# First stage of a decoder layer: squared norms taken in pairs on two column strips, the last chunk reordered, and the loads of the second heads moved to the sync queue

## The chip, the cores and the metric

The kernel runs on one core of a Trainium2 chip. The metric is the device time of one launch in microseconds (us), lower is better. The core has TensorE (matmul, PE), VectorE (DVE), ScalarE (ACT), GpSimd (POOL) and SyncE (SP). They run side by side and meet at semaphores. SP and ACT also issue DMAs here, each on a queue of its own; the data is moved by 16 DMA engines.

## What is computed

One post-norm decoder layer on x of shape (4, 1024, 256): self-attention with a positional bias, cross-attention to 77 context rows, and a top-2 of 8 experts block, each followed by a residual and a layer norm. What matters here is the first stage, the projections of the self-attention:

```python
qkv = jnp.einsum('bsd,ed->bse', x, Wqkv)
q, k, v = jnp.split(qkv, 3, axis=-1)          # 16 heads of 16
logits = jnp.einsum('bihd,bjhd->bhij', q, k) * scale + pos_bias[None]
attn = jax.nn.softmax(logits, axis=-1)
```

The softmax needs an upper bound of each logit in place of its true maximum. The kernel uses |q|·max|k|: for every query row the norm of q (the "norm row" that is stored beside q), and one maximum of |k| over all keys, turned into a shift row of the keys.

## The kernel before

The first stage (`front`) goes over 4096 tokens in eight chunks of 512 (`CH`, c = 0 to 7). In each chunk TensorE computes four units (`unit(c, u)`, line 312): u = 0, 1 are the two halves of K, u = 2, 3 the two halves of Q, each 128 rows by 512 tokens with two accumulation steps, in float32. Each unit has a PSUM bank of its own (`ps_u[u]`). It is drained like this:

- ScalarE copies it to bfloat16 (`parts[u][:, 0]`, "hi", line 434), squares it (`squares[u]`, line 435), and VectorE subtracts hi from it (`rest[u]`, line 502). ScalarE turns the rest to bfloat16 ("mid", line 385), GpSimd takes what is left ("lo", line 585). The mid of a unit comes after the hi and the square of the next one (`finish`).
- SyncE stores hi, mid and lo of each unit to `kstack` or `qstack` (line 229). The hi copy of the same unit of the next chunk waits until all these stores have landed (`unit_stored[u]`).
- TensorE sums the squares by head with a small bfloat16 matmul, `norm(c, u)` (line 322): `members` (128 x 8) are its weights, the squares its 512 moving columns, 8 partitions of PSUM its output. For K, VectorE takes the maximum over the 512 tokens (`key_peak`, line 507); for Q, ScalarE takes the root (line 388) and SyncE stores it as the norm row of 8 partitions (line 233). There are two PSUM banks for norms, `ps_n[u % 2]`, so K and Q take turns in each.

TensorE's order in a chunk is: unit 0, extra work (`fills(c, 0)`, small matmuls of the positional table and of the cross-attention), unit 1, norm 0, unit 2, `fills(c, 1)`, norm 1, unit 3, norm 2, V of the first 256 tokens (`values(c, 0)`, line 339), norm 3, V of the others (`values(c, 1)`). VectorE copies the V results out (`copy_values`, line 513), and SyncE stores them (line 238).

The last chunk also closes the bound on the keys. VectorE writes an early shift row into both key buffers (`early_rows`, line 542, two instructions on one partition with 4096 elements each), then takes the last maxima, the maximum of all (line 560); TensorE turns it over (`key_bound`, line 347), VectorE reduces it (line 571), TensorE spreads it (`spread_bound`, line 352), ScalarE takes the root (line 444), VectorE makes the shift row (lines 575, 577). `key_bound` stands ahead of `values(7, 0)` and `spread_bound` ahead of `values(7, 1)` in TensorE's order.

Self-attention follows without a barrier, head group by head group, 8 steps of 128 keys for each 512 queries. Its first step needs the queries, keys and values of the first heads, the root of the key bound, and free PSUM; the second step on VectorE, ScalarE and GpSimd after that (s = 2) waits for `front_stored`, that is, until all of the first stage's stores have landed. Its output banks `ps_o` are zeroed by VectorE at its start (line 738); they lie where the banks of the norms were.

ScalarE's queue also issues the loads that prefetch the attention (`prefetch(c, u)`): the bias strips and factors in chunks 2 to 5, the seven query loads of the first heads (lines 66 and 84) in (5, 3), their six key loads in (6, 1), their values in (6, 3); and of the second heads the queries in (7, 1), the keys and the values in (7, 3).

## Time and profile before

| | us |
|---|---|
| median of 3 runs | 1292.52 (1290.61 to 1292.66) |
| the profiled execution, its own time | 1292.1 |
| its span in the trace | 1289.9 |
| first stage: TensorE's first matmul to the end of its last `values` | 7.44 to 131.35 |
| TensorE busy over the whole span | 1180.4 (92%) |
| VectorE, ScalarE, GpSimd busy | 860.3, 794.2, 775.4 |

The first stage is a tenth of the span. The engine shares over the whole span are an average over self-attention, cross-attention, routing and experts, so the first stage is read by itself: in stretches of one chunk, each from TensorE's first matmul of the chunk to that of the next.

### The profile page before, as it was taken

How to read it: one execution, taken by the hardware profiler on the slowest of the kernel's cores; microseconds unless marked ns; L12 is line 12 of the kernel's file. 1: busy time of each engine (PE TensorE's matmuls, PEld its weight loads, DVE VectorE, ACT ScalarE, POOL GpSimd, SP SyncE). 2: the span in 40 equal slices, each digit the busy share in tenths (PEclk: the TensorE clock that was granted, in tenths of full speed). 3: DMA queues.
4: the chain of work that ended last, by engine and by line, in shares of the span. 5: the costliest groups of instructions: out<-in, count | busy, mean ns of one | idle time of the engine just before them, and what ended most of it. 6: DMA issues, size and time to landing. Idle time of an engine off the chain costs nothing.

```text
span 1289.9 us, 28208 instructions
## 1 busy us (share of the span) xinstructions
PE 1180.4 (92%) x10751; PEld 682.3 (53%) x10751; DVE 860.3 (67%) x1473; ACT 794.2 (62%) x948; POOL 775.4 (60%) x516
## 2 busy tenths in 40 slices
PE   7999999999999999999899999439999999999980
PEld 3444233333333333332345453339999999999980
DVE  3454789999989999998557886724444444444445
ACT  4555799999999999999376657302222222222224
POOL 1233688878888788888246887734445444444433
PEclk9999899999999999999899999669999999999995
DMA  7699645485559553462277862977777777777748
GB/s 223 201 318 287 235 76 76 76 259 85 90 88 270 83 88 84 71 136 73 84 181 195 216 182 99 188 237 237 243 240 244 235 235 236 245 239 244 237 111 264
DMA packets 134222, 232.51 MB, mean 180 GB/s; under 512 B 31609, under 2 KB 80542, under 8 KB 133766
## 3 DMA queue, kind: packets, MB, share of 16 engines
q1 hardware_dynamic: 102432, 178.10, 46.9%
q0 software_dynamic: 25024, 39.74, 16.4%
q10 hardware_dynamic: 6630, 12.82, 3.4%
q8 instruction: 90, 1.47, 0.5%
q14 instruction: 46, 0.38, 0.1%
HBM read 103.91 MB, written 52.76 MB: 121 GB/s over the span
## 4 chain that ended last, share of the span: by engine, by line
PE 68%; DVE 13%; POOL 5%; issue 5%; ACT 4%; DMA 2%; SPq 0%; ACTq 0%; DVEq 0%; POOLq 0%
PE xp_ps_h L2421 20%; PE xp_ps_y L2433 9%; PE sa_sum L711 9%; PE sa_o L725 9%; DVE sa_probs L759 8%; PE sa_factor L711 4%; PE qp_ps L312 4%; POOL sorted L1136 2%; PE qp_ps L339 2%; ACT sa_probs L783 1%; PE cb_misc L1290 1%; PE cb_l L1305 1%; DVE sa_o_out L745 1%; PE xp_ps_x L2410 1%; ACT fi_rows L2547 1%
## 5 line engine op out<-in xcount | busy, mean ns | idle before, releaser
L807 POOL TENSOR_TENSOR sa_probs<-sa_probs,sa_factors 128x1024 f32<-128x1024 f32 x160 | 383.8, 2399 | 98.0 <-ACT sa_probs L777 98.0
L759 DVE TENSOR_TENSOR sa_probs<-sa_sum,sa_strips 128x1024 f32<-128x1024 f32 x352 | 413.0, 1217 | 44.0 <-PE sa_sum L711 43.7
L783 ACT ACTIVATE sa_probs<-sa_probs 128x1024 f32<-128x1024 f32 (+1 forms) x256 | 342.9, 1384 | 1.2 <-DVE sa_probs L759 1.2
L2421 PEld LDWEIGHTS xp_ps_h<-arena,big 128*128 128x128 f32 x2272 | 266.2, 193 | 5.1 <-ACT arena L2451 1.6
L2421 PE MATMUL xp_ps_h<-arena,big 128*128 128x128 f32 x2272 | 266.8, 276 | 0.9 <-ACT arena L2451 0.9
L725 PE MATMUL sa_o<-sa_probs,sa_v 128*17 128x512 f32 x2048 | 265.7, 594 | 0.8 <-POOL sa_probs L807 0.6
L2389 POOL DMA_INDIRECT y_sum<-stage,xp_place_of x71 | 114.4, 1612 | 190.7 <-DVE xp_weight_of L2480 89.2
L711 PE MATMUL sa_sum<-sa_qk 97*32 97x512 bf16 x2816 | 201.7, 383 | 12.0 <-DVE sa_probs L759 5.2
L711 PEld LDWEIGHTS sa_sum<-sa_qk 97*32 97x32 bf16 x2816 | 63.4, 95 | 230.2 <-DVE sa_probs L759 129.9
L777 ACT ACTIVATE sa_probs<-sa_factor 128x1024 f32<-128x1024 f32 x160 | 164.1, 1026 | 7.0 <-PE sa_factor L711 7.0
L2433 PE MATMUL xp_ps_y<-big,arena 128*128 x568 | 134.5, 380 | 1.3 <-DVE arena L2488 1.3
L2461 ACT ACTIVATE stage<-arena,xp_weight_of 128x256 f32<-128x256 f32 x71 | 36.1, 508 | 129.1 <-DVE arena L2497 129.1
L2433 PEld LDWEIGHTS xp_ps_y<-big,arena 128*128 128x128 f32 x568 | 102.4, 190 | 12.7 <-issue 1.7
L2451 ACT ACTIVATE arena<-xp_ps_x 128x256 f32<-128x256 f32 x71 | 27.2, 383 | 123.7 <-PE xp_ps_x L2410 123.7
L711 PE MATMUL sa_factor<-sa_qk 97*32 97x512 bf16 x1280 | 98.5, 384 | 0.3 <-ACT sa_probs L777 0.3
L2479 DVE CAST xp_place_of<-arena 128x1 uint32<-128x1 f32 x71 | 10.9, 154 | 131.5 <-PE xp_ps_h L2421 131.5
L2378 POOL DMA_INDIRECT arena<-sorted,ro_row_of x71 | 70.2, 989 | 40.3 <-issue 27.5
L585 POOL TENSOR_TENSOR qp_parts<-qp_rest,qp_parts 128x512 bf16<-128x512 f32 x32 | 36.9, 1157 | 89.9 <-ACT qp_parts L385 89.9
L725 PEld LDWEIGHTS sa_o<-sa_probs,sa_v 128*17 128x17 f32 x2048 | 55.8, 99 | 58.4 <-ACT sa_probs L783 3.6
L2482 DVE TENSOR_TENSOR arena<-xp_ps_h,arena 128x1024 f32<-128x1024 f32 x71 | 86.2, 1214 | 0.0
L2455 ACT ACTIVATE arena<-arena 128x512 f32<-128x512 f32 x71 | 44.8, 631 | 65.1 <-DVE arena L2482 65.1
L1470 ACT ACTIVATE big<-cb_l,arena 77x1024 f32<-77x1024 f32 x64 | 68.4, 1106 | 25.4 <-PE cb_l L1305 21.6
(249 smaller groups left out, 1284.9 us busy)
## 6 DMA issues: line engine op xcount, KB each, us to landing
big<-big SPq DMA_DIRECT2D x142, 512.0 KB
sa_strips<-line SPq DMA_DIRECT2D x3, 3840.0 KB, 16.5
sa_qk<-qstack SPq DMA_DIRECT2D x84, 128.0 KB
sa_qk<-kstack SPq DMA_DIRECT2D x84, 128.0 KB
oT<-sa_o_out SPq DMA_DIRECT2D x32, 256.0 KB, 2.4
kstack<-qp_parts SPq DMA_DIRECT2D x48, 128.0 KB, 3.8
qstack<-qp_parts SPq DMA_DIRECT2D x48, 128.0 KB
sa_factors<-factor_line SPq DMA_DIRECT2D x3, 1920.0 KB, 20.5
```

The costliest lines, as they stand in the source:

```text
L711: last = nc.tensor.matmul(into[c * KEYS:(c + 1) * KEYS, a, :], k[m % 2][:, h, at:at + KEYS], q[m % 2][:, h, ih * CH:(ih + 1) * CH], start= ...
L725: last = nc.tensor.matmul(ps_o[n % 2][32 * h:32 * h + VW, :], v[m % 2][:, jt, VW * h:VW * (h + 1)], probs[s % RING][:, h, :], start=(jt == ...
L759: nc.vector.tensor_tensor(probs[s % RING][:, 2 * half:2 * half + 2, :], ps_sum[sums_before(s, half) % 2][:, :, :], strips[hg % 2][:, 2 * h ...
L777: nc.scalar.activation(probs[s % RING][:, 2:4, :], ps_factor[:, :, :], ACT.Exp, scale=0.25).then_inc(factor_exp, 1)
L783: nc.scalar.activation(probs[s % RING][:, 0:heads, :], probs[s % RING][:, 0:heads, :], ACT.Exp, scale=0.25).then_inc(exp_done, 1)
L807: nc.gpsimd.tensor_tensor(probs[s % RING][:, 2:4, :], probs[s % RING][:, 2:4, :], factors[hg % 2][:, :, c1 - CH:c1][:, :, ::-1], ALU.mult) ...
L1470: nc.scalar.activation(pT[:, first:first + 3:2, :], ps_l[use % 2][:NK, :, :], ACT.Exp, bias=neg_shift[:NK, 0:1], scale=HD ** -0.5).then_in ...
L2378: pool.indirect_dma_start(out=x[s % XRING][:, 0:ROW].bitcast(I32), out_offset=None, in_=io["sorted"], in_offset=bass.IndirectOffsetOnAxis( ...
L2389: pool.indirect_dma_start(out=io["y_sum"], out_offset=bass.IndirectOffsetOnAxis(place_of[:, s:s + 1], 0), in_=y[s % 2][:, :], in_offset=No ...
L2421: last = nc.tensor.matmul(ps_h[parity % 2][:, n, m * P:(m + 1) * P], w_now[s % WRING][:, n, k, m * P:(m + 1) * P], xT[parity % 2][:, k, :] ...
L2433: last = nc.tensor.matmul(ps_y[parity % 2][:, 0:D], g[parity % 2][:, k, :], w2[:, e, k, :], start=(k == 0), stop=(k == KH - 1))
L2482: nc.vector.tensor_tensor(h[i][:, :, :].rearrange("p n (m c) -> p (n m) c", c=P), ps_h[i][:, :, :].rearrange("p n (m c) -> p (n m) c", c=P ...
```

## The change

Four things are altered together, all in the first stage and at its seam with the attention.

1. Norms by pairs. `members` becomes 128 x 32 (its pattern repeated), and `norm(c, j)` does the two units 2j and 2j+1 in two matmuls to partitions 0 to 31 and 32 to 63 of one bank `ps_n[j]`, K in bank 0 and Q in bank 1. One `reduce_max` and one root, each over 64 partitions, take the place of two. TensorE's order becomes unit 0, fills, unit 1, unit 2, norm 0, fills, unit 3, V first part, norm 1, V second part. The norm rows of both Q halves are stored after all parts of unit 3.
2. In the last chunk VectorE takes the maximum of all right after its one key maximum, writes one early row before and one after `subtract(7, 2)`, and reduces the turned maximum before `subtract(7, 3)`.
3. The attention's output banks are allocated outside both stages and shared with the norms. They are zeroed by VectorE in the last chunk, after the last root; the shift row follows, and then `copy_values(7, 1)`, which before stood ahead of both.
4. The loads of the second heads (queries, keys, values: 14 DMAs) are issued by SyncE after `front_stored` and ahead of the wait for the shift row, and no longer by ScalarE in chunk 7.

```diff
-        members = sb("members", [P, 8], BF16)
+        members = sb("members", [P, 32], BF16)
-        norms = [sb(f"norms{u}", [8, CH], BF16) for u in range(2)]
+        norms = sb("norms", [64, CH], BF16)
-        ps_n = [ctx.enter_context(nc.psum_tensor(f"qp_norm{u}", [P, CH], F32)) for u in range(2)]
+        ps_n = sa["ps_o"]
@@ SyncE, store(c)
-                    if u >= 2:
-                        sp.wait_ge(root_done, 2 * c + u - 1)
-                        sp.dma_start(dst[NORM_ROW * 8:NORM_ROW * 8 + 8, bass.ts(c, CH)],
-                                     norms[u - 2][:, :]).then_inc(unit_stored[u], 16)
+                sp.wait_ge(root_done, c + 1)
+                for i in range(2):
+                    sp.dma_start(io["qstack"][i][NORM_ROW * 8:NORM_ROW * 8 + 8, bass.ts(c, CH)],
+                                 norms[32 * i:32 * i + 8, :]).then_inc(unit_stored[2 + i], 16)
@@ TensorE
-            def norm(c, u):
-                pe.wait_ge(sq_done, 4 * c + u + 1)
-                if u >= 2:
-                    pe.wait_ge(peak_done, 2 * c + u - 1)
-                elif c >= 1:
-                    pe.wait_ge(root_done, 2 * (c - 1) + u + 1)
-                nc.tensor.matmul(ps_n[u % 2][0:8, :], members[:, :], squares[u][:, :],
-                                 start=True, stop=True).then_inc(norm_ready, 1)
+            def norm(c, j):
+                pe.wait_ge(sq_done, 4 * c + 2 * j + 2)
+                if c >= 1:
+                    pe.wait_ge((peak_done, root_done)[j], c)
+                for i in range(2):
+                    last = nc.tensor.matmul(ps_n[j][32 * i:32 * i + 32, :], members[:, :], squares[2 * j + i][:, :],
+                                            start=True, stop=True)
+                last.then_inc(norm_ready, 1)
                 unit(c, 1)
-                norm(c, 0)
                 unit(c, 2)
+                norm(c, 0)
                 fills(c, 1)
-                norm(c, 1)
                 unit(c, 3)
-                norm(c, 2)
                 if c == NCH - 1:
                     key_bound()
                 values(c, 0)
-                norm(c, 3)
+                norm(c, 1)
@@ ScalarE
-                if u >= 2:
-                    act.wait_ge(norm_ready, 4 * c + u + 1)
-                    nc.scalar.activation(norms[u - 2][:, :], ps_n[u % 2][0:8, :], ACT.Sqrt).then_inc(root_done, 1)
+                if u == 3:
+                    act.wait_ge(norm_ready, 2 * c + 2)
+                    nc.scalar.activation(norms[:, :], ps_n[1][0:64, :], ACT.Sqrt).then_inc(root_done, 1)
-                elif (c, u) == (7, 1):
-                    rows_stored(1)
-                    load_queries(act, io, sa, 1)
-                elif (c, u) == (7, 3):
-                    load_keys(act, io, sa, 1)
-                    load_values(act, io, sa, 1)
@@ VectorE, in the loop over c
                 subtract(c, 1)
                 if c == NCH - 1:
-                    early_rows()
-                key_peak(c, 0)
+                    early_shift()
+                    early_row(0)
+                key_peak(c)
+                if c == NCH - 1:
+                    dve.wait_ge(peak_done, NCH)
+                    nc.vector.reduce_max(k_top[0:64, 0:1], k_peak[:, :], AXX).then_inc(bound_done, 1)
                 subtract(c, 2)
                 drains(c, 1)
-                key_peak(c, 1)
                 if c == NCH - 1:
-                    dve.wait_ge(peak_done, 2 * NCH)
-                    nc.vector.reduce_max(k_top[0:8, 0:1], k_peak[:, :], AXX).then_inc(bound_done, 1)
+                    early_row(1)
+                    dve.wait_ge(kmax_mm, 1)
+                    nc.vector.reduce_max(k_top[0:1, 1:2], ps_u[0][0:1, 0:64], AXX).then_inc(bound_done, 1)
                 subtract(c, 3)
+                copy_values(c, 0)
                 if c == NCH - 1:
                     cross_shift()
-                    dve.wait_ge(kmax_mm, 1)
-                    nc.vector.reduce_max(k_top[0:1, 1:2], ps_u[0][0:1, 0:8], AXX).then_inc(bound_done, 1)
-                for n in range(2):
-                    copy_values(c, n)
...
+                    dve.wait_ge(root_done, NCH)
+                    for bank in ps_n:
+                        nc.vector.memset(bank[:, :], 0.0).then_inc(sa["emptied"], 1)
+                    dve.wait_ge(bound_done, 5)
+                    nc.vector.tensor_scalar(k_top[:, 3:4], k_top[:, 2:3], -1.05, None, ALU.mult).then_inc(bound_done, 1)
+                    dve.wait_ge(bound_done, 6)
+                    nc.vector.tensor_scalar(sa["shift_row"][ROWS:ROWS + 1, :], ones_row[ROWS:ROWS + 1, 0:S],
+                                            k_top[ROWS:ROWS + 1, 3:4], None, ALU.mult).then_inc(bound_done, 1)
+                copy_values(c, 1)
@@ self_attention, SyncE
+            load_queries(sp, io, sa, 1)
+            load_keys(sp, io, sa, 1)
+            load_values(sp, io, sa, 1)
             sp.wait_ge(sa["bound_done"], 7)
             load_bias(1)
@@ self_attention, VectorE
-            for n in range(2):
-                nc.vector.memset(ps_o[n][:, :], 0.0).then_inc(emptied, 1)
```

The waits of `key_bound` and of the first attention steps are as before; the turned maximum is 64 wide instead of 8.

## Rows read from the trace of the kernel before

**Rows 1.** Windows, chunks 5 and 7: length, busy by engine, PEclk, DMA share, GB/s

```profile
86.75:99.74 12.99, 12.99 (x42) 6.16 (x41) 5.58 (x10) 6.46 (x13) 3.47 (x3) 1.00 1.01 347
112.81:131.35 18.54, 15.94 (x41) 7.85 (x39) 8.88 (x14) 9.17 (x17) 5.56 (x6) 0.83 1.04 260
```

**Rows 2.** Waits of TensorE, 0 to 135 us: total, times, longest

```profile
PE qp_norm L322 <- DVE qp_k_peak L507: 1.6, 1, 1.6
PE qp_ps L347 <- DVE qp_k_top L560: 1.0, 1, 1.0
```

**Rows 3.** Timeline of TensorE, chunk 7: start, length, instructions, idle before

```profile
112.81 3.60 PE L312 MATMUL qp_ps<-qp_x,qp_w 128*128 128x512 f32 x8
116.34 0.38 PE L322 MATMUL qp_norm<-qp_squares,qp_members 128*8 128x512 bf16 x1
116.65 1.98 PE L312 MATMUL qp_ps<-qp_x,qp_w 128*128 128x512 f32 x4
118.56 0.38 PE L322 MATMUL qp_norm<-qp_squares,qp_members 128*8 128x512 bf16 x1
```

**Rows 4.** Timeline, TensorE in the attention, eight matmuls on four column strips

```profile
168.54 0.60 PE L711 MATMUL sa_factor<-sa_qk 97*32 97x512 bf16 x8
168.97 1.03 PE L725 MATMUL sa_o<-sa_probs,sa_v 128*17 128x512 f32 x8
```

**Rows 5.** Timeline of TensorE, end of chunk 7

```profile
122.42 0.38 PE L322 MATMUL qp_norm<-qp_squares,qp_members 128*8 128x512 bf16 x1 [1.57 <-DVE qp_k_peak L507]
123.95 2.73 PE L339 MATMUL qp_ps<-qp_w,qp_x 128*128 128x256 f32 x8
127.64 3.78 PE L339 MATMUL qp_ps<-qp_w,qp_x 128*128 128x256 f32 x8
```

**Rows 6.** Windows of 1 us around both falls of the clock, columns as in Rows 1

```profile
126.00:127.00 1.00, 1.00 (x3) 0.08 (x1) 0.28 (x1) 0.60 (x1) 0.00 (x0) 0.50 1.08 277
134.00:135.00 1.00, 0.00 (x0) 0.00 (x0) 1.00 (x1) 0.00 (x0) 0.89 (x1) 1.00 0.05 17
136.00:137.00 1.00, 0.83 (x12) 0.30 (x12) 1.00 (x2) 0.21 (x1) 0.47 (x1) 0.50 0.73 123
```

**Rows 7.** Timeline of VectorE, chunk 7 and the seam

```profile
118.35 3.21 DVE L542 TENSOR_SCALAR sa_qk<-qp_ones_row,qp_k_early 1x4096 bf16<-1x4096 bf16 x2
121.60 0.68 DVE L507 TENSOR_REDUCE qp_k_peak<-qp_norm 8x1 f32<-8x512 f32 x1
131.46 0.69 DVE L513 COPY qp_v_out<-qp_ps 128x512 f32<-128x512 f32 x1 [4.06 <-PE qp_ps L339]
132.84 1.02 DVE L738 MEMSET sa_o<- 128x512 f32 x2
133.90 4.80 DVE L759 TENSOR_TENSOR sa_probs<-sa_sum,sa_strips 128x1024 f32<-128x1024 f32 x4
```

**Rows 8.** Timeline of ScalarE: chunk 5, a wait and its followers; chunk 7

```profile
91.59 0.60 ACT L434 ACTIVATE qp_parts<-qp_ps 128x512 bf16<-128x512 f32 x1 [1.38 <-DMA kstack<-qp_parts]
92.09 0.59 ACT L435 ACTIVATE qp_squares<-qp_ps 128x512 bf16<-128x512 f32 x1
120.14 0.60 ACT L434 ACTIVATE qp_parts<-qp_ps 128x512 bf16<-128x512 f32 x1 [2.09 <-issue]
```

**Rows 9.** Timeline of SyncE's queue, stores of the norm rows of chunk 4

```profile
85.73 0.41 SPq L233 DMA_DIRECT2D qstack<-qp_norms  x1
88.18 0.34 SPq L233 DMA_DIRECT2D qstack<-qp_norms  x1
```

**Rows 10.** Landing of line 229's K stores; DMA issues at 87 to 90, 128 to 133

```profile
DMA to landing us min/median/max: 1.9/3.8/8.4
...
kstack<-qp_parts SPq DMA_DIRECT2D x1, 128.0 KB, 7.0
...
vpad<-qp_v_out SPq DMA_DIRECT2D x2, 272.0 KB, 4.2
```

**Rows 11.** Timeline of GpSimd, the first product of the attention

```profile
134.11 2.36 POOL L807 TENSOR_TENSOR sa_probs<-sa_probs,sa_factors 128x1024 f32<-128x1024 f32 x1 [5.85 <-ACT sa_probs L777]
```

49 lines of the change are left out of this document (23 added, 26 removed).

## Prediction

> **What bounds the kernel now.** I read the change first, to know which stretch it can touch (the first stage and its seam with the attention), and then the windows by chunk [rows 1]. The reader is to see that in chunk 5 TensorE's busy time is the whole length of the stretch (12.99 of 12.99), while VectorE, ScalarE and GpSimd are at half of it or less. Chunks 0 to 4 and 6 look the same; only chunk 7 has idle TensorE time (15.94 of 18.54) and a mean granted clock of 0.83. Next the waits of TensorE [rows 2]: over the whole first stage it waits for an engine only twice, 1.6 and 1.0 us, both in chunk 7. So in chunks 0 to 6 a microsecond that TensorE doesn't spend is a microsecond of the end time, as long as nothing else becomes late; in chunk 7 the chain through VectorE counts too. The other number to watch is the DMA share, 1.01 in chunk 5 and 1.04 in chunk 7: the 16 engines have no room there, and this is where the cover may fail. Later stages start from semaphores and not from a date, so I carry a gain of the first stage to the end unchanged.
>
> **What one norm costs.** Two units back to back and the step to the norm take 116.34 - 112.81 = 3.53 us [rows 3]. Eight matmuls of 0.43 us make 3.44, so 0.09 is the step into the narrow matmul. The norm takes 116.65 - 116.34 = 0.31. The unit behind it takes 118.56 - 116.65 = 1.91, and of that 0.09 is again the step into the next norm, so 0.10 beyond 1.72 is the step out. One norm costs 0.09 + 0.31 + 0.10 = 0.50 us of TensorE. Four a chunk: 2.0.
>
> **What a pair costs.** It has one step in, one step out, and two streams of 512 columns. Bounds: if the two strips run together it costs what one does, 0.50; if one after the other, the second adds a stream of 0.21 (half of a float32 matmul's 0.43). The nearest row has bfloat16 matmuls of 512 columns on four column strips: eight start at 168.54 and the next line's at 168.97, 0.43 for two rounds of four [rows 4]. Strips run together there, at 0.21 a round, and I take 0.02 for the second strip: 0.52. A pair of norms saves 2 x 0.50 - 0.52 = 0.48, two pairs a chunk 0.96, and chunks 0 to 6 give 7 x 0.96 = 6.7 us (serial strips: 4.0).
>
> The Trainium skill ("TensorE: Matmul & The Clock Gate", the table of measured speedups in the part on packing small matmuls) has a less perfect figure for column strips: three strips of 512 columns ran 2.38 times as fast as one by one, 1.26 of a single one's time. By that a pair would cost some 0.05 us more than I take, an estimate from that page, and the sum would lose under 1 us. The rows of this kernel show no such loss, and the sum keeps to them.
>
> **What else of the pairs is free, and its cover.** The pair needs the second unit's squares. They end about 1.1 us after the unit (hi at 91.59, square 92.09 to 92.68 [rows 8]), and a unit of 1.72 lies between: covered, by 0.5. The pair for Q has `values(c, 0)` as the same cover. Eight roots and eight key maxima (0.68 us each [rows 7]) go away, on engines that are not the bound: nothing. Their replacements run over 64 partitions instead of 8 with the same 512 elements each, so I give them the same length.
>
> **The stores of the norm rows, where I see a loss.** Before, the row of unit 2 is issued ahead of unit 3's parts (85.73) and that of unit 3 behind them (88.18) [rows 9], 1.0 before and 1.4 us after chunk 5 begins at 86.75. Now both go last, that of unit 2 at about +1.4. The hi copy of unit 2 in the next chunk waits for this row, and it is due earlier than before: three units (5.2) and the fill of chunk 5 (0.6, what 12.99 leaves beside six times 1.72 and four norms [rows 1]), about +5.8. That leaves 4.4 us to land. A store of a K part lands in 3.8 us in the median, which fits; one issued at 87 to 90 took 7.0, and the longest 8.4 [rows 10]. So in chunk 5 I expect the hi copy at about +8.3, 2.5 us late. Queued behind it on ScalarE are square 2, mid 1, hi 3 and square 3, half a microsecond apart: square 3 ends at 8.3 + 0.5 x 4 + 0.6 = 10.9. TensorE comes to the Q pair at about +9.8 (four units 6.9, fill 0.6, pair 0.5, V 1.8). It stalls 1.1 us. A wait for a landing of this kind is already there once, 1.38 us on ScalarE [rows 8]. In chunk 6 the first heads' key loads keep ScalarE to about +7.3 anyway and the landing is near it; I take 0.4 more for chunks 4 and 6 together. Range of this term: 0 to 5 us. I take 1.5.
>
> **Chunk 7, counted from its first matmul (112.81).** Before, two things make VectorE late: ScalarE's six query loads and one row load hold back hi 2 to 120.14 [rows 8], and the two early rows take 3.21 us ahead of the key maximum (121.60 [rows 7]). TensorE waits twice for this [rows 2], and then its clock is 0.50 instead of 1.00 [rows 6]: `values` take 2.73 and 3.78 where 1.99 is usual [rows 5]. It ends at 131.35, +18.5, and the attention's first add starts at 133.90, +21.1.
> After: TensorE does units 0 to 2 (5.2), the pair (to 5.6), unit 3 (to 7.5). VectorE has subtract 1 until 5.4, the early shift 0.15, one early row 1.6 (to 7.15), the key maximum to 7.85, the maximum of all to 8.05. `key_bound` starts there: TensorE waits 0.6. Then V first part to 10.0, the Q pair to 10.5. VectorE has meanwhile subtract 2 (8.7), the other early row (10.35), the turned maximum (10.5), and `spread_bound` waits 0.1 at most. V second part: 10.8 to 12.7. So TensorE saves 18.5 - 12.7 = 5.8: 2.6 - 0.7 of idle time, 2.9 of low clock (0.8 + 1.9 in `values`, the rest in the small ones), and 1.0 of norms.
> VectorE goes on with subtract 3 (11.3), V copy (11.9), then waits for the last root. ScalarE has mid 3 at 11.4 to 12.0 and the root to 12.5. Zeroing takes 1.02 [rows 7], to 13.5; the key root is ready at 12.7; the shift row 0.6, to 14.2; the second V copy 0.7, to 14.9. The first add starts at about +14.95. The seam is 2.2 us after TensorE's end where it was 2.5. The gain to the first add is 21.1 - 14.95 = 6.1 us.
>
> **Who waits for the V copy.** It was the first of this row of steps and is now the last. The first factor scores of TensorE and the last V store wait for it. The scores come at +15.0, about when the first add starts; before, they came ahead of it. Their exponential (1.0) and GpSimd's product (2.36 [rows 11]) end near +19, and TensorE wants them with the values of step 0 at about +20: covered by 1 us. The store takes about 4.2 to land [rows 10], so `front_stored` comes at about +19; three adds of 1.2 end at +18.6. A new wait of 0.4 (0 to 1.5) on VectorE.
>
> **The second heads' loads.** What they cost ScalarE in chunk 7 is counted above. On SyncE they stand behind `front_stored` and ahead of the shift row's wait and of the bias of head group 1. 14 issues of some 0.5 are 7 us, so they are out at about +26, and step 16 wants them 30 us after the first add, +45. The bias is wanted at step 64. SyncE's first output store is due at about +38. Nothing: covered by over 10 us each. The DMA engines do the same work, only later.
>
> **Start of the attention.** Before, TensorE idles at 133 to 135 us and the clock falls again [rows 6]. It still has about 1.5 to 2 us idle between +13.3 and +15. I expect one fall there as before: no difference; 2 us less if it doesn't come.
>
> **Sum.** -6.7 (pairs) + 1.5 (rows that land late) - 6.1 (chunk 7 and seam) + 0.4 (`front_stored`) = -10.9 us. The profiled execution's own time is 1292.1 (span 1289.9 and 2.2 around it), 0.4 below the median of the runs, so 1292.1 - 10.9 = 1281.2, and 1281.6 against the median. I give 1281.5.
>
> **The rivals.**
> - A: the DMA engines take more of it back. For it: the share over 1.0 [rows 1] and 7.0 us to landing, while every chunk is now 1 us shorter. If chunks 4 to 7 stall 1 to 1.5 us each, the term is 5: 1285. Against: ScalarE has about 1.5 us of slack before TensorE feels it. Chance 0.18.
> - B: strips one after another, or dearer steps in and out because of the 32-column weights. 2.7 us less, 1 more in chunk 7: 1284.5 to 1285. Against: [rows 4]. Chance 0.07.
> - C: chunk 7 still trips the clock. TensorE's idle 0.7 there is small beside the 2.6 that stood before the fall, but if ScalarE or a landing makes it 2, the 2.9 us stay and 1 or 2 of idle time with them: 1285 to 1286. Chance 0.12.
> - D: better than the sum. No late rows (1.5) and no fall at the start of the attention (2): 1278. Chance 0.15.
> - E, slower than before: the late rows drag the clock down. Place: hi of unit 2 in chunks 4 to 7. If every norm row took 8.4 us (the longest landing [rows 10]), the hi copy would be 4 us late, TensorE would stall 2.4, as long as the 2.6 before the fall in chunk 7, and the stretch behind it would run at half clock, which cost 2.9 there. Four times 5.3 is 21, less 12.8: +8, 1300. It decides from a stall of about 2 us in three chunks on. Against: the median of 3.8. Chance 0.04.
> - F: it does its part but the end doesn't move, since a later stage waits for something with a date of its own. I see none. Chance 0.03.
>
> **How the numbers follow.** The forecast has 0.41. The range reaches from D without its last half microsecond to A, B and most of C: 1277.5 to 1286, and leaves out E, F and the tails. A difference of 0.2% (2.6 us) is about what a measurement of this kernel can tell. Faster by over 0.2%: all but E, F and a worse form of A or C, 0.91. Within: 0.05. Slower: 0.04.
>
> **What would show it.** The windows by chunk should be near 12.0 us for chunks 5 and 6, with TensorE's norm rows as two matmuls 128*32 starting within 0.05 us of each other. Chunk 7 should take 12.7 with a clock of 1.00. A wait of ScalarE's line 434 for `qstack` stores, or of TensorE's norm for ScalarE's square, in chunk 5 or 6, shows the late rows. On VectorE the order is zeroing, shift row, V copy, first add without gaps. I am wrong if the chunks keep 13 us without TensorE idle (B), if TensorE idles over 1 us in several chunks (A, E), or if the clock row shows 0.50 before +12 of chunk 7 (C).

## The result and the profile after

The changed kernel takes 1280.32 us, median of 7 runs (1278.53 to 1286.26), beside 1292.52 (1290.61 to 1297.39) before: a ratio of 0.991, 95% interval 0.9887 to 0.9932. The forecast was 1281.5 with a range of 1277.5 to 1286.0. The profiled execution took 1281.3 us (span 1279.5), 10.8 less than that of before (1292.1, span 1289.9).

Windows of the changed kernel, chunks 5, 6 and 7, columns as in [rows 1]:

```profile
82.06:94.28 12.22, 12.19 (x41) 6.19 (x40) 4.96 (x9) 5.78 (x11) 3.65 (x4) 1.00 1.03 349
94.28:107.70 13.42, 12.23 (x42) 6.54 (x41) 4.77 (x9) 8.00 (x15) 5.08 (x5) 1.00 1.08 322
107.70:120.95 13.25, 12.29 (x45) 6.28 (x47) 8.97 (x15) 7.87 (x15) 7.13 (x7) 1.00 0.68 226
```

Chunk 5 went from 12.99 to 12.22 with TensorE still busy throughout (12.19). Chunk 6 has 1.2 us without TensorE. Chunk 7 went from 18.54 to 13.25, and its clock is 1.00 where it was 0.83. Its DMA share is 0.68 where it was 1.04.

Timeline of TensorE, chunks 6 and 7 and the seam, beside [rows 3] and [rows 5]:

```profile
100.60 0.39 PE L323 MATMUL sa_o<-qp_squares,qp_members 128*32 128x512 bf16 x2 [0.28 <-ACT qp_squares L429]
105.54 0.39 PE L323 MATMUL sa_o<-qp_squares,qp_members 128*32 128x512 bf16 x2 [0.91 <-ACT qp_squares L429]
...
107.70 5.31 PE L314 MATMUL qp_ps<-qp_x,qp_w 128*128 128x512 f32 x12
112.94 0.39 PE L323 MATMUL sa_o<-qp_squares,qp_members 128*32 128x512 bf16 x2
113.26 1.98 PE L314 MATMUL qp_ps<-qp_x,qp_w 128*128 128x512 f32 x4
116.21 0.27 PE L349 MATMUL qp_ps<-arena,qp_k_top 64*1 64x64 f32 x2 [0.96 <-DVE qp_k_top L553]
116.41 1.99 PE L341 MATMUL qp_ps<-qp_w,qp_x 128*128 128x256 f32 x8
...
118.96 1.99 PE L341 MATMUL qp_ps<-qp_w,qp_x 128*128 128x256 f32 x8
...
122.74 0.61 PE L714 MATMUL sa_factor<-sa_qk 97*32 97x512 bf16 x8 [1.24 <-DVE qp_v_out L507]
```

A pair is one line with x2, and what follows starts 0.32 us later (112.94 to 113.26) where one norm took 0.31. Both `values` of chunk 7 take 1.99 instead of 2.73 and 3.78. The last line is new: the first factor scores wait for the V copy, which now comes last on VectorE.

Timeline of VectorE, chunk 7 and the seam, beside [rows 7]:

```profile
113.23 2.01 DVE L537 TENSOR_SCALAR sa_qk<-qp_ones_row,qp_k_early 1x4096 bf16<-1x4096 bf16 x1
115.28 0.68 DVE L501 TENSOR_REDUCE qp_k_peak<-sa_o 64x1 f32<-64x512 f32 x1
116.00 0.15 DVE L553 TENSOR_REDUCE qp_k_top<-qp_k_peak 64x1 f32<-64x8 f32 x1
...
116.78 1.28 DVE L537 TENSOR_SCALAR sa_qk<-qp_ones_row,qp_k_early 1x4096 bf16<-1x4096 bf16 x1
...
120.36 1.02 DVE L572 MEMSET sa_o<- 128x512 f32 x2 [0.67 <-ACT qp_norms L388]
...
122.71 4.80 DVE L760 TENSOR_TENSOR sa_probs<-sa_sum,sa_strips 128x1024 f32<-128x1024 f32 x4
```

The first add starts 11.19 us earlier than before (133.90 to 122.71). Four adds run without a gap, so VectorE doesn't wait for `front_stored`.

Where the gain arises and where it stays:

| change, us | forecast | measured |
|---|---|---|
| chunks 0 to 6, TensorE's work | -6.7 | -6.3 |
| TensorE's waits in them | +1.5 | +1.2 |
| chunk 7 and the seam, to the first add | -6.1 | -6.1 |
| from the first add to the attention's last output copy | +0.4 | +0.6 |
| from there to the end of the span | 0 | +0.2 |
| sum | -10.9 | -10.4 |

The second row is the two waits above, 0.28 + 0.91; the first is what is left of the -5.1 by which the seven chunks became shorter (105.37 to 100.29). Chunks 1 to 3 are each 1.0 us shorter. Of chunk 0's 0.8 part is chance: the kernel before takes 15.65 us for it, and `kept_busy`, the same code in that chunk, 15.09. Chunk 7 and the seam are 21.09 less 15.01. About half of the 0.6 is lost at the start of the attention, but not where I had put it: VectorE waits for `front_stored` neither before nor after, and idles 2.74 instead of 2.43 us, for TensorE's scores, ahead of its third group of adds. Where the rest is lost I did not find. The last output copy starts at 601.9 instead of 612.5.

### The profile page after: what moved, and what is told of

The parts are those of the page before. It is cut to its first block, busy times and chain, and to the rows that moved or that the text cites. A ratio compares the mean times of both kernels' runs of the same rounds, so it can differ in the third digit from the quotient of the medians.

```text
span 1279.5 us, 28175 instructions
## 1 busy us (share of the span) xinstructions
PE 1169.8 (91%) x10751; PEld 680.3 (53%) x10751; DVE 856.1 (67%) x1465; ACT 790.8 (62%) x940; POOL 775.0 (61%) x516
## 4 chain that ended last, share of the span: by engine, by line
PE 65%; DVE 15%; POOL 6%; issue 6%; ACT 5%; DMA 4%; DVEq 0%; ACTq 0%; SPq 0%; POOLq 0%
PE xp_ps_h L2422 20%; PE xp_ps_y L2434 9%; PE sa_sum L714 9%; PE sa_o L728 9%; DVE sa_probs L760 8%; PE sa_factor L714 4%; PE qp_ps L314 3%; POOL sorted L1137 2%; ACT sa_probs L784 1%; PE qp_ps L341 1%; DMA kstack<-qp_parts 1%; PE xp_ps_x L2411 1%; DVE sa_o_out L746 1%; ACT fi_rows L2548 1%; PE cb_misc L1291 1%
## 5 line engine op out<-in xcount | busy, mean ns | idle before, releaser
L714 PE MATMUL sa_sum<-sa_qk 97*32 97x512 bf16 x2816 | 201.6, 382 | 10.8 <-DVE sa_probs L760 4.0
L2434 PEld LDWEIGHTS xp_ps_y<-big,arena 128*128 128x128 f32 x568 | 102.4, 190 | 12.7 <-issue 1.7
L2480 DVE CAST xp_place_of<-arena 128x1 uint32<-128x1 f32 x71 | 10.9, 154 | 128.4 <-PE xp_ps_h L2422 128.4
```

The lines of the kernel that those rows point to most:

```text
L714: last = nc.tensor.matmul(into[c * KEYS:(c + 1) * KEYS, a, :], k[m % 2][:, h, at:at + KEYS], q[m % 2][:, h, ih * CH:(ih + 1) * CH], start= ...
L2434: last = nc.tensor.matmul(ps_y[parity % 2][:, 0:D], g[parity % 2][:, k, :], w2[:, e, k, :], start=(k == 0), stop=(k == KH - 1))
```

## Experiments

In the experiments a difference of 1 us is read from dates in the trace and not from one time, for a reason that the runs gave themselves (last section). The dates are TensorE's first matmul and that of chunk 7, and, counted from the latter, the end of the last `values`, VectorE's first add of the attention and its last output copy.

| kernel | chunks 0 to 6 | chunk 7 to V end | to the first add | to the last output copy | span |
|---|---|---|---|---|---|
| before | 105.37 | 18.6 | +21.09 | +499.7 | 1289.9 |
| after | 100.29 | 13.25 | +15.01 | +494.2 | 1279.5 |
| pairs_only | 100.54 | 16.7 | +19.21 | +499.8 | 1283.3 |
| unpaired | 105.41 | 14.5 | +16.58 | +495.5 | 1285.7 |
| old_order | 100.91 | 20.1 | +22.52 | +501.5 | 1287.5 |
| loads_back | 100.73 | 14.1 | +16.43 | +498.7 | 1282.7 |
| same_strip | 101.81 | 14.0 | +16.03 | +494.9 | 1282.0 |
| kept_busy | 104.82 | 15.7 | +18.18 | +497.5 | 1287.8 |
| k_parts_twice | 103.43 | 13.25 | +15.01 | +494.1 | 1290.5 |
| keys_later | 99.42 | 13.25 | +15.01 | +494.1 | 1278.7 |
| rows_own_sem | 99.42 | 14.9 | +16.65 | +495.7 | 1280.8 |
| v_first | 98.69 | 13.25 | +15.72 | +494.8 | 1285.4 |
| rows_late | 100.94 | 12.2 | +15.27 | +494.3 | 1285.3 |
| all_three | 102.32 | 12.2 | +15.27 | +494.1 | 1287.4 |

The column of chunks 0 to 6 has a spread of its own: `after`, `pairs_only`, `old_order`, `loads_back`, `v_first` and `rows_late` have the same code there and take 98.69 to 100.94 us. A difference of under 2 us in this column is no finding. The last output copy, counted from chunk 7, is steadier: `after`, `k_parts_twice`, `keys_later`, `rows_late` and `all_three` lie between +494.1 and +494.3.

The theory: two gains that add up, one from TensorE doing less in chunks 0 to 6, one from chunk 7, where less idle time also keeps TensorE's clock up. The rivals: that the strips save little by themselves, that the fall of the clock isn't caused by the idle time, and that it is the loads, not VectorE's order, that mend chunk 7.

### The two halves apart

`pairs_only` keeps the pairs and takes back the loads and VectorE's order; `unpaired` is the other half on the kernel before.

```diff
 # pairs_only, against the changed kernel
                     early_row(0)
+                    early_row(1)
                 key_peak(c)
...
+                elif (c, u) == (7, 1):
+                    rows_stored(1)
+                    load_queries(act, io, sa, 1)
+                elif (c, u) == (7, 3):
+                    load_keys(act, io, sa, 1)
+                    load_values(act, io, sa, 1)
```

> The pairs alone: norms on two column strips in TensorE's new order, but VectorE's old order in chunk 7 (both early rows ahead of the key maximum, zeroing at the very end) and the second heads' loads on ScalarE. My theory (the gain has two separate sources, pairs in chunks 0 to 6, and VectorE's order in chunk 7): chunk 7 begins near 107.7 us as in the changed kernel, 5.1 ahead of before; in chunk 7 TensorE reaches the key bound at +7.5 and waits about 2.7 us for the rows and the maximum, its clock falls to 0.50, and the first add of the attention comes at about 127 to 128 us (changed kernel 122.7, before 133.9). Time about 1286. Rival 1 (the pairs also mend chunk 7, since fewer steps wait on each other): clock stays at 1.00, first add near 123.5, time 1281. Rival 2 (DMA engines give nothing back without the other edits): chunk 7 begins later than 109.

Measured: 1287.35 us (1285.38 to 1291.05, 10 runs), ratio 0.996 (0.9941 to 0.9979). TensorE waits 2.75 us for the key bound, its clock is 0.50 for 3.4 us, and the first add starts at 127.27, 6.6 earlier than before.

> All but the pairs: VectorE's new order in chunk 7, zeroing there and the second heads' loads on SyncE, norms one by one as before. My theory: chunk 7 begins at 112.8 us as before; in it TensorE waits under 1.5 us in all, the clock stays at 1.00, V ends at about +14, and the first add comes at about +16, near 128.8 us; time about 1287.5. Together with the pairs alone the two gains should add up to that of the changed kernel within 1 us. Rival (the order only works with one key maximum a chunk): TensorE waits over 2 us, the clock falls, first add near 132, time 1291.

Measured: 1288.73 us (1286.01 to 1293.41, 10 runs), ratio 0.9977 (0.9962 to 0.9993). TensorE waits 0.36 and 1.03 us in chunk 7, the clock stays at 1.00, and the first add starts at 128.74, 5.2 earlier than before. Of that 0.7 is not the edit's: TensorE's first matmul came at 6.75 in this execution and at 7.44 before. Counted from each execution's first matmul, the two halves give 6.7 + 4.5 = 11.2 at the first add, and both together 11.2 too. At the last output copy it is 4.7 + 4.2 = 8.9 beside 10.6, so there they don't simply add. The pairs bring their 4.8 in chunks 0 to 6 alone; behind chunk 7's first matmul `pairs_only` is where the kernel before was (+499.8 and +499.7), since it loses at the start of the attention what it gains to the first add (its clock is 0.50 there for 10.2 us, from 128.9). The other half is what chunk 7 gives (+495.5).

### Which part mends chunk 7

`old_order` has the pairs and the loads on SyncE, with VectorE's steps as before.

```diff
                     early_row(0)
+                    early_row(1)
                 key_peak(c)
-                if c == NCH - 1:
-                    dve.wait_ge(peak_done, NCH)
-                    nc.vector.reduce_max(k_top[0:64, 0:1], k_peak[:, :], AXX).then_inc(bound_done, 1)
                 subtract(c, 2)
...
```

> The changed kernel with VectorE's old order in chunk 7 (both early rows ahead of the key maximum, the maximum of all after subtract 2, turned maximum, V copies, shift row, zeroing last), loads still on SyncE. My theory (order is what counts): TensorE waits over 2 us at the key bound, clock 0.50 behind it, first add at 126 to 127.5. Rival (loads are what counts): wait under 1.5, clock 1.00, first add before 124.5.

Measured: 1289.27 us in one run. The first add comes at 131.39, later than I expected by about 4 us. TensorE's and VectorE's timelines of `old_order`:

```profile
120.07 0.37 PE L349 MATMUL qp_ps<-arena,qp_k_top 64*1 64x64 f32 x2 [3.65 <-DVE qp_k_top L556]
```

```profile
114.41 4.11 DVE L537 TENSOR_SCALAR sa_qk<-qp_ones_row,qp_k_early 1x4096 bf16<-1x4096 bf16 x2
118.56 0.68 DVE L501 TENSOR_REDUCE qp_k_peak<-sa_o 64x1 f32<-64x512 f32 x1
```

The two early rows take 4.11 us here, where they took 3.21 before and 3.22 in `pairs_only`. GpSimd's timeline has the difference: in `pairs_only` one of its subtractions overlaps the rows, and the next starts at 117.27, behind them; in `old_order`, where no loads hold ScalarE back, the next starts at 115.91, ahead of the second row, and both rows are slowed (last section). So TensorE idles 3.65 us and its clock is 0.50 for 10.2 us, over both `values`. Moving the loads doesn't mend chunk 7 by itself; both early rows ahead of the key maximum keep TensorE idle. How much each of VectorE's other new places brings (the maximum of all, the turned maximum, the zeroing) no run shows singly.

`loads_back` is the changed kernel with the second heads' loads issued by ScalarE in chunk 7 as before (the same lines as in `pairs_only`, and the three calls on SyncE removed).

> The changed kernel with the second heads' loads back on ScalarE's queue in chunk 7. My theory (the key maximum now stands ahead of subtract 2, so ScalarE's issue time no longer reaches it): hi of unit 2 starts 2 us later, but the key bound of TensorE comes within 0.3 us of the changed kernel's and the clock stays at 1.00; the first add comes 0 to 0.8 us later, 122.7 to 123.5. Rival (ScalarE's loads were what held chunk 7 back): first add at 125 or later and the clock at 0.50 in chunk 7.

Measured: 1284.69 us in one run. The wait for the key bound is the same (0.95), the clock stays at 1.00, but two other waits appear. TensorE, then VectorE of `loads_back`:

```profile
120.59 0.38 PE L354 MATMUL qp_ps<-qp_k_top,arena 1*128 1x1 f32 x2 [0.82 <-DVE qp_k_top L565]
...
132.71 1.04 PE L717 MATMUL sa_factor<-sa_qk 97*32 97x512 bf16 x8 [3.38 <-ACT sa_probs L781]
```

```profile
131.64 2.35 DVE L763 TENSOR_TENSOR sa_probs<-sa_sum,sa_strips 128x1024 f32<-128x1024 f32 x2 [2.97 <-SPq L255]
```

L255 is the end of SyncE's waits for the stores, behind which it gives `front_stored`. Windows of `loads_back` (first fence) and of the changed kernel from the last V stores on, then the landing of these two stores in `loads_back` and in the changed kernel:

```profile
124.00:128.00 4.00, 2.08 (x32) 0.68 (x36) 3.94 (x5) 2.17 (x3) 0.90 (x1) 1.00 1.21 224
```

```profile
122.00:126.00 4.00, 2.54 (x36) 0.79 (x40) 3.97 (x4) 1.97 (x2) 1.36 (x1) 0.85 0.47 160
```

```profile
vpad<-qp_v_out SPq DMA_DIRECT2D x2, 272.0 KB, 6.2
```

```profile
vpad<-qp_v_out SPq DMA_DIRECT2D x2, 272.0 KB, 2.3
```

The loads take room from the last stores: 6.2 instead of 2.3 us to land, share 1.21 instead of 0.47. All fourteen traces agree on this: the last V stores land in 2.2 to 2.4 us in the ten kernels that load from SyncE afterwards, and in 4.2 to 6.2 us in the four with the loads on ScalarE in chunk 7 (before 4.2, `pairs_only` 4.4, `kept_busy` 5.3, `loads_back` 6.2). Besides, the V stores are issued 1.5 us later in chunk 7 (+15.8 instead of +14.35), as ScalarE's copies come later behind its own loads (hi of unit 2 at +7.6 instead of +5.35). Counted from chunk 7 the last output copy is at +498.7 where the changed kernel has +494.2. Moving the loads is no neutral part of the change, as I had called it: with the new order on VectorE it is worth 4.5 us, and without it nothing is gained (`old_order` +501.5, `pairs_only` +499.8). The span is only 3.2 us longer, because the later stages took 2.3 us less in this execution (last section).

### What the strips are worth

`same_strip` keeps the order of the pairs but puts both norms on strip 0, each in a bank of its own, with two maxima and two roots.

```diff
-                    last = nc.tensor.matmul(ps_n[j][32 * i:32 * i + 32, :], members[:, :], squares[2 * j + i][:, :],
+                    last = nc.tensor.matmul(ps_n[i][0:32, :], members[:, :], squares[2 * j + i][:, :],
```

> The changed kernel with both matmuls of a norm pair on the same column strip (partitions 0 to 31), each in a bank of its own, so that they can't run together; two key maxima and two roots a chunk again. My theory (the second strip is free because strips run together): the two matmuls start 0.21 us apart instead of less than 0.02, each pair costs TensorE 0.2 more, and chunk 7 begins 14 x 0.21 = 2.9 us later, near 110.6. Rival (what is saved is only the steps in and out of the narrow matmuls, strips add nothing): chunk 7 begins within 0.7 us of the changed kernel's 107.7.

Measured: 1284.1 us in one run. Timeline of TensorE, chunk 0 of `same_strip`:

```profile
15.42 0.61 PE L325 MATMUL sa_o<-qp_squares,qp_members 128*32 128x512 bf16 x2
15.96 0.40 PE L268 MATMUL qp_ps<-qp_combined,qp_ramp 101*128 101x16 f32 x2
```

From pair to next work 0.54 us, with two strips 0.32: the second norm costs 0.22 on the same strip and 0.01 on its own. Over 14 pairs that is 3.1 us. Chunks 0 to 6 are 1.5 us longer than with two strips, and TensorE waits 0.7 less in them, so 2.2 of these 3.1 are seen in the sum; but that sum has the spread named above. Chunks 1 to 3, where TensorE waits in neither kernel, show it better: 15.5, 15.5 and 17.7 us instead of 15.1, 15.1 and 17.1, so 0.4 to 0.5 each, of the 1.0 that the pairs save in each. The strips are worth nearly half of what a pair saves (0.22 of 0.49); the other 0.27 comes from joining two norms, with one step in and one out instead of two, and one strip saves that as well.

### Is it the idle time that lowers the clock?

`kept_busy` is the kernel before, with three more matmuls in the gaps of chunk 7. They compute nothing that is used.

```diff
                 unit(c, 3)
+                if c == NCH - 1:
+                    pe.wait_ge(v_copied, 2 * c - 1)
+                    pe.wait_ge(spare_drained, len(SPARE))
+                    for k in range(2):
+                        nc.tensor.matmul(ps_u[4][:, :], w[:, k, 0:P], x[1][:, k, :], start=(k == 0), stop=(k == 1))
                 norm(c, 2)
                 if c == NCH - 1:
+                    nc.tensor.matmul(ps_u[4][:, :], w[:, 0, 0:P], x[1][:, 0, :], start=True, stop=True)
                     key_bound()
```

> The kernel before, with matmuls of no use (2 and 1 float32 ones of 512 columns into a free bank that V overwrites later) where TensorE waited 1.6 and 1.0 us in chunk 7; nothing else is altered. My theory (idle time is what takes the clock to 0.50, and it costs 2.9 us there): the clock stays at 1.00 to the end of V, TensorE ends V at 128.5 to 129.3 instead of 131.35, the first add comes at 131.0 to 132.0 instead of 133.9, and the time is some 2 to 3 us lower. Rival (the clock falls for another reason): V takes 2.7 and 3.8 us as before and the time is the same or higher.

Measured, the window of chunk 7 and the timelines of TensorE and VectorE of `kept_busy`:

```profile
112.13:127.80 15.67, 15.67 (x51) 7.36 (x53) 8.89 (x14) 8.30 (x16) 5.54 (x6) 1.00 1.07 289
```

```profile
123.30 1.99 PE L339 MATMUL qp_ps<-qp_w,qp_x 128*128 128x256 f32 x8
...
125.84 1.99 PE L339 MATMUL qp_ps<-qp_w,qp_x 128*128 128x256 f32 x8
```

```profile
134.51 2.36 DVE L765 TENSOR_TENSOR sa_probs<-sa_sum,sa_strips 128x1024 f32<-128x1024 f32 x2 [0.71 <-SPq L253]
```

With work in the gaps TensorE has no idle time in chunk 7, the clock is 1.00 throughout, both `values` take 1.99 and the first add comes at +18.18 instead of +21.09: 2.9 us, the price of the low clock in the prediction. Part of it is lost again in the attention, where VectorE waits 0.71 us for `front_stored`: +497.5 at the last output copy, 2.2 less than before. The time can't be told from no change: 1289.74 (1286.14 to 1293.91, 10 runs), ratio 0.9986 (0.9967 to 1.0006).

### What delays the squares in chunk 6

TensorE's 0.28 and 0.91 us there go back to ScalarE. Waits of ScalarE in the changed kernel to 135 us (total, times, longest):

```profile
ACT qp_parts L428 <- DMA kstack<-qp_parts: 6.6, 4, 3.2
...
ACT qp_parts L428 <- DMA qstack<-qp_norms: 1.0, 1, 1.0
```

I had forecast the second line. In this execution it is the first that is long: the stores of the K parts, 1.4 before. But that is one execution. In the others with the same chunks 0 to 6 ScalarE waits, for K parts and for norm rows in this order, 4.0 and 0.7 us (`pairs_only`), 0 and 1.9 (`old_order`), 1.2 and 4.5 (`loads_back`), 0 and 0.4 (`v_first`), 2.8 and 3.4 (`rows_late`). The norm rows are the longer wait in four of the six. With the chunks of before (the kernel before, `unpaired`, `kept_busy`) it is 0.9 to 1.5 us, all for K parts, and TensorE never waits for a square. Chunk 5 of `loads_back` is the forecast's picture, a hi copy of unit 2 at +8.5 behind a norm row, and TensorE's wait at the Q pair. ScalarE, then TensorE:

```profile
91.05 0.60 ACT L434 ACTIVATE qp_parts<-qp_ps 128x512 bf16<-128x512 f32 x1 [2.32 <-DMA qstack<-qp_norms]
```

```profile
93.68 0.39 PE L323 MATMUL sa_o<-qp_squares,qp_members 128*32 128x512 bf16 x2 [1.19 <-ACT qp_squares L435]
```

Besides, ScalarE issues the six key loads in chunk 6 (99.53 to 102.81 in the changed kernel), and its next hi copy starts at 102.92. Three kernels, of one run each, take one of these causes away each. `k_parts_twice` gives both K units two buffers in turn (with a wait for GpSimd added to VectorE's subtraction, which keeps `rest` safe):

```diff
+        def slot(c, u):
+            return u if u >= N_PARTS - 4 or c % 2 == 0 else 4 + u
...
+                    if u < N_PARTS - 4:
+                        if c >= 2:
+                            act.wait_ge(unit_stored[slot(c, u)], per_unit[u] * (c // 2))
...
```

> The changed kernel with a second set of part buffers for the two K units, so that the hi copies of K wait for the stores of two chunks back. My theory (TensorE's 1.2 us of waits for squares in chunk 6 come from stores that land late): ScalarE no longer waits for K stores, and TensorE waits at most 0.4 us in chunks 0 to 6; chunk 7 begins at 106.5 to 107.0. Rival (they come from the six key loads that ScalarE issues in chunk 6): the wait at the Q pair of chunk 6 stays at 0.7 or more.

Measured: 1292.71 us in one run. Timeline of TensorE and a wait of ScalarE, `k_parts_twice`:

```profile
96.73 0.39 PE L327 MATMUL sa_o<-qp_squares,qp_members 128*32 128x512 bf16 x2 [2.88 <-ACT qp_squares L436]
```

```profile
ACT qp_parts L435 <- DMA qstack<-qp_norms: 6.4, 3, 2.6
```

The wait for K stores is gone, and the one for the norm rows is long, at about the total that the K parts had (6.4 and 6.6). TensorE waits 4.4 us in three places, more than in any of the six executions above (0.4 to 1.9). So this remedy fails: ScalarE only comes to another late store.

`keys_later` issues the first heads' keys in (6, 3) and their values in (7, 1):

```diff
-                elif (c, u) == (6, 1):
-                    load_keys(act, io, sa, 0)
                 elif (c, u) == (6, 3):
+                    load_keys(act, io, sa, 0)
+                elif (c, u) == (7, 1):
                     load_values(act, io, sa, 0)
```

> The changed kernel with the first heads' six key loads issued half a chunk later (after square 3 of chunk 6 instead of after square 1) and the values' load in chunk 7. If ScalarE's issue time in chunk 6 is the cause of TensorE's waits for squares, the wait at the Q pair of chunk 6 (0.9) goes to 0.2 or less. If late landings are, it stays over 0.5. In either case the attention begins no later; over all the first add comes 0 to 0.9 us earlier than 122.7.

Measured: 1280.52 us in one run. One wait of TensorE's norms is left, the K pair's:

```profile
100.34 0.39 PE L323 MATMUL sa_o<-qp_squares,qp_members 128*32 128x512 bf16 x2 [0.51 <-ACT qp_squares L429]
```

The 0.91 of the Q pair is gone, and nothing came for it. In chunk 6 TensorE waits at the Q pair in all eight kernels that have the pairs on two strips and the key loads in (6, 1), 0.30 to 1.02 us, and in neither of the two that issue them later (`keys_later`, `all_three`), so that wait does hang on the key loads, or on them and a late store together. What it is worth is less sure: chunks 0 to 6 are 0.9 shorter and the span 0.8 (1278.7), and both lie within the spread; `v_first`, with the key loads in their old place, has 98.69. This one run can't be told from the changed kernel by its time.

`rows_own_sem` counts the norm rows on a semaphore of their own, which the root waits for and no longer the hi copy of a Q unit:

```diff
-                                 norms[32 * i:32 * i + 8, :]).then_inc(unit_stored[2 + i], 16)
+                                 norms[32 * i:32 * i + 8, :]).then_inc(norm_stored, 16)
...
+                    if c >= 1:
+                        act.wait_ge(norm_stored, 32 * c)
                     nc.scalar.activation(norms[:, :], ps_n[1][0:64, :], ACT.Sqrt).then_inc(root_done, 1)
```

> The changed kernel with a semaphore of their own for the norm rows' stores: the root of the next chunk waits for it and the hi copies of Q no longer do. My theory of the prediction (the norm rows, now stored last, are what makes TensorE wait for squares): ScalarE waits for no norm row, TensorE waits 0.4 us at most in chunks 0 to 6, and chunk 7 begins at 106.5 to 107.0. Rival (the landing of K's stores ahead of the hi copies of K, and ScalarE's key loads): TensorE's wait for squares in chunk 6 stays at 0.9 us or more.

Measured: 1282.59 us in one run. Timeline of TensorE in chunks 6 and 7, and a wait of ScalarE:

```profile
105.51 0.39 PE L325 MATMUL sa_o<-qp_squares,qp_members 128*32 128x512 bf16 x2 [0.30 <-ACT qp_squares L433]
...
114.06 0.39 PE L325 MATMUL sa_o<-qp_squares,qp_members 128*32 128x512 bf16 x2 [1.09 <-ACT qp_squares L433]
117.80 0.27 PE L351 MATMUL qp_ps<-arena,qp_k_top 64*1 64x64 f32 x2 [1.43 <-DVE qp_k_top L557]
```

```profile
ACT qp_parts L432 <- DMA kstack<-qp_parts: 5.8, 3, 3.6
```

The waits for norm rows are gone, chunk 6 waits only 0.30, and 1.09 stands at the K pair of chunk 7 and 0.5 more at the key bound. Chunk 7 is 1.6 longer, which is more than the 0.9 (within the spread) by which chunks 0 to 6 are shorter.

### The order at the seam

`v_first` puts the second V copy ahead of the zeroing, so that TensorE's first factor scores don't wait.

```diff
                     cross_shift()
+                    copy_values(c, 1)
                     dve.wait_ge(root_done, NCH)
...
```

> The changed kernel with the last V copy ahead of zeroing and shift row again, as before the change. My theory (VectorE sets the seam): TensorE's wait of 1.2 us at the first factor scores goes, but VectorE has to wait for TensorE's V (until +13.2) before it can zero, so the first add comes 0.3 to 0.8 us later than +15.0 after the start of chunk 7. Rival (TensorE's and ScalarE's earlier start of the factor path is worth more): the first output copy of the attention comes earlier than 23.3 us after the first add and makes up for it.

Measured: TensorE's wait for the copy falls from 1.24 to 0.24 us, but the first add starts 0.7 later (+15.72), and the first output copy comes 23.08 us after it instead of 23.30. Only 0.2 of the 0.7 is made up, and the last output copy is at +494.8 instead of +494.2: the copy is better last.

`rows_late` writes both early rows later, to free the key bound.

```diff
                     early_shift()
-                    early_row(0)
                 key_peak(c)
...
-                    early_row(1)
+                    early_row(0)
                     dve.wait_ge(kmax_mm, 1)
...
+                    nc.vector.memset(ps_n[0][:, :], 0.0).then_inc(sa["emptied"], 1)
+                    early_row(1)
                     dve.wait_ge(root_done, NCH)
```

> The changed kernel with the first early row behind subtract 2 of chunk 7 instead of ahead of the key maximum, one output bank zeroed early and the second early row behind it. Theory: the key bound of TensorE comes without a wait (1.0 us in the changed kernel), and the first add at +14.0 after the start of chunk 7 instead of +15.0. Rival (the rows only move the work on VectorE, which is the bound anyway): TensorE's wait goes, but the first add stays within 0.3 us of +15.0.

Measured: the wait at the key bound is gone and TensorE ends chunk 7 a microsecond earlier (+12.2), but the first add starts at +15.27. TensorE only waits longer behind it:

```profile
122.87 0.61 PE L714 MATMUL sa_factor<-sa_qk 97*32 97x512 bf16 x8 [2.52 <-DVE qp_v_out L507]
```

The last output copy is where it was (+494.3). At the seam the first add hangs on VectorE's steps (here without a gap from the second early row on) and, in the changed kernel, on the last root, and no longer on TensorE's end.

`all_three` is `rows_own_sem`, `keys_later` and `rows_late` in one kernel, to look for something better than the change.

> The changed kernel with three edits together: own semaphore for the norm rows, the first heads' key loads half a chunk later, the early rows later. Chunk 7 begins at about 106.3 us with TensorE waiting under 0.5 us for squares, the first add comes at +14.0, near 120.4, and the time is 2 us under that of the changed kernel, about 1278. If the three work against each other (the key loads now meet the rows' copies in ScalarE's queue) the first add is at 121.5 or later.

Measured: 1282.84 us (1280.86 to 1289.29, 6 runs), ratio to the kernel before 0.9931 (0.9907 to 0.9956). Its seven chunks took 102.32 with three waits of 0.87, 0.46 and 1.34 us. No gain over the change is seen, whose ratio is 0.991 (0.9887 to 0.9932).

## Why the prediction was right, point by point

- **A norm costs 0.50, a pair 0.52.** Right: chunks 1 to 3 are each 1.0 us shorter, by 0.96 in the forecast. Over seven chunks it is 6.3 instead of 6.7, since chunks 4 to 6 give 0.8 to 0.9 each and chunk 0 varies by itself. The row of the attention's strips [rows 4] gave the price of the second strip: I took 0.02, and it is 0.01. The table of measured speedups in the Trainium skill ("TensorE: Matmul & The Clock Gate", "Measured speedup vs the span model") has three strips at 2.38 times the speed of one by one, by which a pair would cost some 0.05 more, an estimate from that page; the trace doesn't bear that out here, since a pair takes 0.32 where a single norm took 0.31.
- **1.5 us for norm rows that land late.** The size was right (1.2 in the changed kernel's trace, 0.4 to 1.9 in the six with these chunks), and the mechanism is there, but it is half of the story. Late norm rows are the longer wait in four of the six; in the changed kernel's own trace the stall stood elsewhere, in chunk 6 and mostly at the Q pair, and the K parts were what landed late (6.6 us of ScalarE's waiting, norm rows 1.0). Two steps failed. One is "in chunk 6 the key loads keep ScalarE to about +7.3 anyway": they didn't only cover a wait, they were part of one (`keys_later` has none at that place). The other is that I followed only the stores whose issue the change moved. When every chunk is 1 us shorter, all landings are due sooner, those of the K parts too. Freeing one kind of store shows the other: with K buffered twice the norm rows are late, with the norm rows freed the K parts are. That the sum's term matched to 0.3 us in this one trace is luck within its spread.
- **Rival A.** Its mechanism is there, at the size of the forecast. ScalarE's slack, which I held against it, took up most of the waiting: 7.6 us on ScalarE became 1.2 on TensorE.
- **Chunk 7.** TensorE's end was forecast at +12.7 and came at +13.25; the first add at +14.95 and +15.01. The term that was too small is the early row, 1.6 us forecast and 2.01 measured. I had halved the 3.21 of two rows, but of these the first overlapped a GpSimd subtraction (118.12 to 119.27) and the second didn't; the row that counts is the slow one. That makes TensorE wait 0.96 instead of 0.6 at the key bound. It hardly reached the first add, which hangs on the last root, as the forecast had it: the zeroing starts at +12.66 (12.5 forecast) behind a wait of 0.67 for that root.
- **The clock, rival C.** Right, and shown: `kept_busy` fills the gaps and gets back the 2.9 us that the sum has for it. Chunk 7 still has 0.96 us of idle time and keeps 1.00, as did `unpaired` with 0.36 and 1.03. With 1.57 and 1.03 (before), 2.75 (`pairs_only`) and 3.65 (`old_order`) it fell.
- **The new order of the V copy.** The factor scores wait 1.24 us for it, as foreseen, and that is nearly free: with 0.24 of it left `v_first` is 0.6 us slower by the last output copy.
- **`front_stored`, +0.4.** Wrong: nothing waits for it. I gave the last V store 4.2 us, as it took before [rows 10]; it lands in 2.3. SyncE goes on at 125.26, and four adds run through to 127.5.
- **The second heads' loads, "nothing".** Wrong, though covered in the forecast's sum. The step that failed is "the DMA engines do the same work, only later". It is the same work, but in chunk 7 it stood beside the last stores, for which the attention waits: `loads_back` has 6.2 instead of 2.3 us to land, and waits of 0.82 us at `spread_bound` and 2.97 at `front_stored`. The first is in my term for chunk 7 all the same, since I had counted ScalarE free of these issues there; the second is why the +0.4 didn't appear. The forecast came out right with a part called neutral that brings 4.5 us: without the moved loads 3.7 us are lost between the first add and the last output copy (`loads_back`), where the sum has 0.4.
- **Start of the attention, "one fall as before".** Right in number, slightly late: the clock falls at 124.8, 2.1 us after the first add instead of 1.4. Windows of the changed kernel:

```profile
124.00:125.00 1.00, 0.61 (x8) 0.11 (x8) 1.00 (x2) 1.00 (x2) 0.36 (x1) 0.88 0.59 199
125.00:126.00 1.00, 0.88 (x12) 0.34 (x16) 1.00 (x2) 0.43 (x1) 1.00 (x1) 0.50 0.00 0
```

- **The end moves by what the first stage gives.** Right in the main: 11.2 at the first add, 10.6 at the last output copy, 10.4 at the end.

What stays open: how much of the landing times in chunks 4 to 6 is the shorter chunk and how much differs from one execution to the next. The waits of TensorE's norms sum to 0.4 to 1.9 us in kernels with the same chunks 0 to 6 (`pairs_only`, `loads_back`, `old_order`, `v_first`, `rows_late`), so a single trace doesn't fix that term to better than about 1 us. It is open too why the two halves give 1.7 us less by the last output copy than the change does, when they add up at the first add.

## What to carry to other kernels

When a saturated stage is made faster by cutting the bound engine's work, go through every transfer that must land before a buffer is used again, not only those that the edit moves; they all come due sooner, and freeing one kind can leave the next as late. Which one is late differs between executions of the same code, so look at several traces before naming the culprit. A load that nobody wants soon still costs if it is issued beside the last stores of a stage for which the next one waits. Count an instruction's steps around it too, here 0.19 of 0.50 us for a narrow matmul between wide ones: joining two norms saved 0.27 us before the second strip saved 0.22.

## What the runs showed of the hardware

**VectorE and GpSimd hold each other up.** An early row (one partition, 4096 elements in bfloat16) takes 1.28 us when it starts ahead of GpSimd's subtraction and 2.01 when it starts behind it. GpSimd's lo subtraction takes 1.15 and up to 1.59. Timeline of GpSimd, changed kernel, to be read beside the two rows at 113.23 and 116.78 above:

```profile
113.01 1.15 POOL L585 TENSOR_TENSOR qp_parts<-qp_rest,qp_parts 128x512 bf16<-128x512 f32 x1 [3.60 <-ACT qp_parts L385]
114.73 1.53 POOL L585 TENSOR_TENSOR qp_parts<-qp_rest,qp_parts 128x512 bf16<-128x512 f32 x1 [0.56 <-ACT qp_parts L385]
117.49 1.59 POOL L585 TENSOR_TENSOR qp_parts<-qp_rest,qp_parts 128x512 bf16<-128x512 f32 x1 [1.23 <-ACT qp_parts L385]
```

Each time the one that started first keeps its length and the other is longer: GpSimd at 113.01 against the row at 113.23 (+0.73), the row against GpSimd at 114.73 (+0.38), the row at 116.78 against GpSimd at 117.49 (+0.44). The Trainium skill ("SBUF — State Buffer", "SBUF: two separate sides") says that the two share a pair of ports which whoever starts first holds for its whole instruction, on VectorE's side for some kinds of instruction only. The trace agrees in order and size: the three overlaps are 0.93, 0.51 and 0.57 us long, and the later one is longer by 0.73, 0.38 and 0.44.

**Four of the fourteen profiled executions lose some 6 us in the cross-attention**, 500 us behind the change. Windows of the changed kernel and of `rows_late`:

```profile
620.00:630.00 10.00, 8.89 (x38) 4.33 (x40) 3.46 (x3) 4.43 (x6) 4.04 (x4) 0.84 0.00 0
630.00:640.00 10.00, 9.04 (x56) 4.28 (x52) 4.69 (x10) 6.11 (x6) 0.00 (x0) 1.00 0.30 91
```

```profile
620.00:630.00 10.00, 9.55 (x32) 4.01 (x30) 2.34 (x3) 3.83 (x6) 4.41 (x4) 0.70 0.00 0
630.00:640.00 10.00, 8.39 (x32) 4.13 (x32) 3.76 (x6) 3.75 (x4) 0.00 (x0) 0.66 0.20 59
```

Summed over windows of 10 us from 600 to 720, the clock is at 0.50 for 24 to 27 us in `v_first`, `rows_late`, `all_three` and `k_parts_twice`, and for 7 to 14 us in the ten others (10.4 in the changed kernel and in `old_order`). From the last output copy to the end these four take 683.3 to 684.7 us; eight others take 677.1 to 678.2, and `pairs_only` and `loads_back`, with 6.8 us at 0.50, 675.2 and 675.4. The runs of one kernel split likewise: six of the changed kernel lie between 1278.5 and 1281.8, one is at 1286.3; of `all_three` four lie at 1280.9 to 1283.3 and two at 1288.4 and 1289.3. So two single times of this kernel can lie 8 us apart for a reason that isn't in the change, which gives 10 to 12. Why an execution falls on one side wasn't tried.
